# A short block packed with 128 columns, a projection moved ahead of packing, one transfer for two h0 blocks, and the last normalisation on GpSimd

## The chip, the core and the metric

The kernel runs on one core of a Trainium2 chip. The metric is the device time of that core in microseconds (us). Three runs of the kernel before the change gave 470.95, 471.35 and 472.15 us; their median is 471.35 us. A separate profiled execution took 470.71 us, of which 468.9 us lie between its first and its last instruction (its span).

## The reference, cut to what matters

Inputs: features x (5000 x 128), an adjacency matrix adj (5000 x 5000, f32, about 100 MB, zeros and ones), h0 (5000 x 128), one-hot classes y (5000 x 16), two 128 x 128 weights and two biases.

```
# layer 0
a   = adj * (y @ y.T)                     # keep edges inside a class
a   = a / max(sum(|a|, row), 1e-12)
x   = layernorm(x + 0.9 * (a @ x) + 0.1 * h0)
# layer 1
f   = tanh(adj * adj) * (adj > 0)         # a row has fewer than 350 ones: top_k keeps all
h2  = tanh(x @ W_proj + b_proj)
x   = layernorm(x + relu(f @ (h2 @ W_gcn) + b_gcn))
```

## The kernel before

The 5000 rows are 39 full blocks of 128 rows and a short one of 8 (`NB` = 40 blocks, `FULL` = 39, `LAST` = 39, `TAIL` = 8). The 5000 columns are cut in the same way. Blocks 1 to 38 come in pairs: of 256 consecutive rows, lane p holds rows 2p and 2p+1, so that block 2s+1 has the even ones and block 2s+2 the odd ones.

The adjacency is read once, in layer 0, and kept as bits. For each block of rows t, SyncE (SP) loads two halves of the row block into `a_rows` (2688 and 2312 columns, two buffers of each, L314). VectorE (DVE) casts each half to bf16 in `a_bits` (L750; one buffer of each half), ScalarE (ACT) counts its zeros (L644), and TensorE (PE) packs it: in `pack_rows` (L437) the block of 128 x 128 bits is the stationary operand and the 128 x 9 matrix `pack` moves, so that 16 rows become one 16-bit word. There are 21 such matmuls for half 0 and 19 for half 1; the last of half 1 has 8 stationary columns and not 128, since the last block of columns has 8. ACT copies the words (L661), DVE masks them with the same-class words (`same_class`, L862) and unpacks them, one bit of each byte at a time, as fp8 weights (`turned`, L839, eight instructions), and PE multiplies them by the parts of x (L487, 40 matmuls of 257 columns in two halves of 21 and 19) into `acc`.

What follows in layer 0 for a block n is: a row scale, two multiply-adds, the statistics (DVE, L880 to L908), the inverse deviation on GpSimd (POOL, `inverse_std`, L394 and L397, a power on 128 x 1), the normalisation (DVE, L851), a copy to `xs` (POOL, L410), a transpose (PE, L542), a copy of it (ACT, L695), the projection (PE, two f32 matmuls, L566), tanh (ACT, L677), and the second product (PE, L550). POOL forms 0.1 * h0 + x beforehand (`residual`, L383 and L388) from `h0_rows`, which SP loads with one transfer for each block, of 128 pieces of 512 bytes (`load_h0`, L321).

The engines run software-pipelined steps. In PE's step t (L512 to L576) the order is: first half of the product of block t-2, packing of half 0 of block t, transpose of block t-5, second product of block t-6, second half of the product of block t-2, packing of half 1 of block t, projection of block t-5. Steps 3 to 12 hold extra matmuls for the same-class words. A helper `steps` writes the first and the last steps out and runs the middle ones in a loop of two steps. SP's step t loads the rows of block t once the cast and the count of block t-2 have freed the buffer (L312, L313), and then h0 of block t-1, which waits until `residual` of block t-3 is through (L320).

Layer 1 unpacks the kept words and multiplies them by the parts of the features (L487, 40 matmuls a block), followed by the same chain to the second normalisation (`step1` of DVE, L1008 on; L851 and the store of the result at L351). Part of its first products is started early, in steps 42 to 45. At the very end each engine reads a flag (`TENSOR_LOAD`: DVE at L1358, SP at L1172) and jumps over a second, general version of the kernel that is not needed here, to the barrier at L1489.

## Time and profile before

| | value |
|---|---|
| median of three runs | 471.35 us (470.95 to 472.15) |
| profiled execution, time | 470.71 us |
| its span | 468.9 us |
| PE busy | 444.4 us, 95% of the span |
| DVE busy | 378.3 us, 81% |
| ACT busy | 266.3 us, 57% |
| POOL busy | 158.9 us, 34% |
| HBM read | 105.57 MB |
| chain that ended last | PE 88%, DVE 6%, ACT 3% |

The page cuts the span into 40 slices. The transfers run at 400 to 420 GB/s for the first 22 slices, which is layer 0, and hardly at all afterwards. So the shares of busy time over the whole span mix two stages: layer 0, to about 283 us, and layer 1, to 462 us, with a tail of 7 us. Matmuls overlap one another, so a busy PE isn't PE at its peak; how far its chain can be shortened is read from the pieces of the chain of work that ended last.

### The profile page before, as it was taken

What the parts mean: (1) busy time and instruction counts of PE and PEld (TensorE: products, weight loads), DVE (VectorE), ACT (ScalarE), POOL (GpSimd) and SP (SyncE); (2) the same over time, 40 slices, a digit from 0 to 9 for tenths busy, and PEclk for the clock granted to TensorE, in tenths of its full rate; (3) what the DMA queues carried; (4) which work ended last, traced back from release to release, by engine and by line L of the source; (5) the groups of instructions that cost most, each with busy time, mean ns of one, the idle gap of its engine ahead of it and who ended that gap; (6) DMA issues with size and microseconds to landing.
All of it is one profiled execution on the core that took longest, in us unless ns stands there. A gap on an engine that the chain in (4) does not pass through costs nothing.

```text
span 468.9 us, 15231 instructions
## 1 busy us (share of the span) xinstructions
PE 444.4 (95%) x5104; PEld 391.6 (84%) x5104; DVE 378.3 (81%) x1362; ACT 266.3 (57%) x355; POOL 158.9 (34%) x309
## 2 busy tenths in 40 slices
PE   3669999999999999999999999999999999999994
PEld 2448889899889989988998887888888888888882
DVE  5888999999999999999999956676566566566553
ACT  4998999999999999999999934900000000000000
POOL 3012543455544444555444441221221221221221
PEclk9977999999999999999999999999999999999999
DMA  8999999999999999999999100000000000000000
GB/s 266 410 413 418 416 415 408 409 396 412 420 420 419 420 421 418 421 421 419 413 418 419 32 1 1 13 12 17 17 11 17 17 11 17 17 11 16 17 17 18
DMA packets 28254, 108.50 MB, mean 231 GB/s; under 512 B 5401, under 2 KB 18226, under 8 KB 18226
## 3 DMA queue, kind: packets, MB, share of 16 engines
q1 hardware_dynamic: 28226, 108.14, 57.4%
q8 instruction: 16, 0.26, 0.2%
q14 instruction: 12, 0.10, 0.1%
HBM read 105.57 MB, written 2.56 MB: 231 GB/s over the span
## 4 chain that ended last, share of the span: by engine, by line
PE 88%; DVE 6%; ACT 3%; issue 2%; POOLq 0%; DVEq 0%; POOL 0%; ACTq 0%
PE acc L487 71%; PE words L437 9%; PE proj_acc L566 3%; PE feat_acc L550 2%; DVE a_bits L750 2%; ACT count_out L651 2%; PE xnt_acc L542 1%; DVE x_parts L779 1%; DVE g_words L300 1%; ACT count_out L720 1%; DVE turned L839 1%; ACT count_out L712 1%; PE gram_acc L469 0%; DVE y_diag L764 0%; PE words L453 0%
## 5 line engine op out<-in xcount | busy, mean ns | idle before, releaser
L487 PE MATMUL acc<-x_parts,turned 128*128 128x257 f16 (+1 forms) x1600 | 195.2, 276 | 0.7 <-DVE x_parts L779 0.7
L644 ACT ACTIVATE count_out<-a_rows,ones 128x2688 bf16<-128x2688 f32 (+1 forms) x80 | 190.0, 2375 | 0.5
L487 PEld LDWEIGHTS acc<-x_parts,turned 128*128 128x128 fp8e4 (+1 forms) x1600 | 156.9, 98 | 25.3 <-DVE x_parts L779 1.2
L487 PE MATMUL acc<-f_parts,turned 128*128 128x256 f16 (+1 forms) x1560 | 171.6, 273 | 0.8 <-DVE turned L839 0.8
L487 PEld LDWEIGHTS acc<-f_parts,turned 128*128 128x128 fp8e4 (+1 forms) x1560 | 152.0, 98 | 19.3 <-issue 1.3
L750 DVE TENSOR_SCALAR a_bits<-a_rows 128x2688 bf16<-128x2688 f32 (+1 forms) x80 | 116.6, 1458 | 2.3 <-DMA a_rows<-in_adj_dram 1.9
L394 POOL TENSOR_TENSOR var_eps<-mean_var,consts 128x1 f32<-128x1 f32 x80 | 18.5, 231 | 269.2 <-DVE mean_var L1046 139.8
L839 DVE TENSOR_SCALAR turned<-a_words 128x320 uint16 (+1 forms) x305 | 66.5, 232 | 53.2 <-PE acc L487 52.8
L397 POOL TENSOR_TENSOR rstd<-var_eps,consts 128x1 f32<-128x1 f32 x80 | 87.4, 1093 | 6.3
L839 DVE TENSOR_SCALAR turned<-same_class 128x320 uint16<-128x320 uint16 x313 | 71.7, 254 | 0.1
L437 PEld LDWEIGHTS words<-pack,a_bits 128*128 128x128 bf16 (+1 forms) x1600 | 53.8, 96 | 10.0 <-DVE a_bits L750 6.4
L437 PE MATMUL words<-pack,a_bits 128*128 128x9 bf16 (+1 forms) x1600 | 54.9, 167 | 5.2 <-DVE a_bits L750 5.2
L851 DVE TENSOR_SCALAR xn<-z,mean_var,rstd 128x128 f32<-128x128 f32 x80 | 30.4, 381 | 1.9 <-POOL rstd L397 1.0
L410 POOL COPY xs<-xn 128x128 f32 (+2 forms) x40 | 28.1, 702 | 0.4 <-DVE xn L851 0.4
L383 POOL TENSOR_TENSOR h_part<-h_rows,consts 128x128 f32<-128x128 f32 (+1 forms) x40 | 19.7, 492 | 20.4 <-DMA h_rows<-in_L_gnn_h_dram 20.2
L661 ACT ACTIVATE a_words<-words 128x360 f32 (+1 forms) x40 | 18.9, 472 | 13.3 <-PE words L437 13.2
L388 POOL TENSOR_TENSOR xh<-h_part,xs 128x128 f32<-128x128 f32 (+1 forms) x40 | 21.4, 534 | 7.4 <-POOL h_part L383 6.6
L566 PE MATMUL proj_acc<-xn_t,wp 128*128 128x128 f32 (+1 forms) x80 | 19.1, 320 | 0.2 <-issue 0.2
L1022 DVE SCALAR_TENSOR_TENSOR low_feat<-acc,consts,bg_all 128x128 f32<-128x128 f32 (+1 forms) x40 | 13.8, 344 | 4.7 <-PE acc L487 4.7
L677 ACT ACTIVATE h_t<-proj_acc,bp_col 128x128 f32<-128x128 f32 (+1 forms) x40 | 14.6, 365 | 5.2 <-PE proj_acc L566 5.2
L695 ACT ACTIVATE xn_t<-xnt_acc 128x128 f32<-128x128 f32 (+1 forms) x40 | 11.0, 275 | 10.3 <-PE xnt_acc L542 8.7
L550 PE MATMUL feat_acc<-wg,h_t 128*128 128x128 f32 (+1 forms) x80 | 15.6, 277 | 0.8 <-ACT h_t L677 0.6
(111 smaller groups left out, 287.8 us busy)
## 6 DMA issues: line engine op xcount, KB each, us to landing
a_rows<-in_adj_dram SPq DMA_DIRECT2D x39, 1344.0 KB, 8.0
a_rows<-in_adj_dram SPq DMA_DIRECT2D x39, 1156.0 KB, 8.3
h_rows<-in_L_gnn_h_dram SPq DMA_DIRECT2D x39, 64.0 KB, 5.6
out_dram<-xn SPq DMA_DIRECT2D x39, 64.0 KB, 1.5
xs<-in_x_dram SPq DMA_DIRECT2D x3, 640.0 KB, 10.3
xs<-in_x_dram SPq DMA_DIRECT2D x1, 512.0 KB, 9.0
y_nat<-in_L_gnn_y_dram SPq DMA_DIRECT2D x1, 304.0 KB, 3.6
a_rows<-in_adj_dram SPq DMA_DIRECT2D x1, 84.0 KB
```

What stands on the lines that cost most here:

```text
L383: pool.tensor_tensor(h0_part[0:m, :], h0_rows[par][0:m, :], alpha[0:m, :].to_broadcast([m, F]), ALU.mult).then_inc(s_h0part, 1)
L388: pool.tensor_tensor(xh[par][0:m, :], h0_part[0:m, :], at(xs, n, m), ALU.add)\
L397: pool.tensor_tensor(rstd[par][0:m, :], var_eps[0:m, :], neg_half[0:m, :], ALU.pow)\
L410: pool.tensor_copy(at(xs, t - 4, m), xn[par][0:m, :]).then_inc(s_kept, 1)
L437: mm = pe.matmul(words[par][0:k, b * PITCH:b * PITCH + WORDS + 1], a_bits[h][0:m, c:c + (k - 1) * d + 1:d], pack[0:m, :], start=True, stop ...
L487: mm = pe.matmul(acc[par][0:m, 0:cols], bits, parts[:, b, 0:cols], start=first and b == blocks[0], stop=last and b == blocks[-1])
L550: pe.matmul(feat_acc[0:m6, 0:F], h2_t[:, 0:m6], wg[:, :], start=True, stop=True)\
L566: pe.matmul(proj_acc[:, 0:m5], wp[:, :], xn_t[:, 0:m5], start=True, stop=True)\
L644: act.activation(count_out[0:m, 0:w], a_rows[par][h][0:m, 0:w], ACT.Relu, bias=ones[0:m, 0:1], scale=-HUGE, accum_out=col).then_inc(s_coun ...
L750: dve.tensor_scalar(a_bits[h][0:m, 0:w], a_rows[par][h][0:m, 0:w], 1.0, None, ALU.is_equal).then_inc(s_bits, 1)
L839: up = dve.tensor_scalar(turned_at(n, par)[:, :, bit * WORDS:(bit + 1) * WORDS], source, abs(shift), ONE_PAIR, op, ALU.bitwise_and)
L851: return dve.tensor_scalar(xn[par][0:m, :], z[par][0:m, :], mean_var[par][0:m, 0:1], rstd[par][0:m, :], ALU.subtract, ALU.mult)
```

## The change

Four things change.

- The last block of columns, in half 1, is packed with 128 stationary columns as the others are. The columns past the 5000th are zeros that DVE writes once into `a_bits[1]`; the memsets of the places that the short product left unwritten go, and with them a wait of PE in the setup.
- In PE's step the projection of block t-5 stands ahead of the packing of half 1 and not behind it.
- h0 of the two blocks of a pair comes with one transfer, of 128 pieces of 1 KB, into a buffer of twice the size. It is issued in even steps, and waits for `residual` of the block four before. For the buffers' names, SP and POOL run their loops four steps at a time (`steps4`).
- The last block's second normalisation is done by POOL, straight after its inverse deviation, and not by DVE.

```diff
+    def steps4(eng, step, lag, first):
+        for t in range(first):
+            step(t, t % 2, t // 2, 0, t)
+        count = (FULL - first) // 4
+        with eng.Fori(0, count) as i:
+            for c in range(first, first + 4):
+                step(i * 4 + c, c % 2, i * 2 + c // 2, i, c)
+        for t in range(first + count * 4, NB + lag):
+            step(t, t % 2, t // 2, 0, t)
...
-        h0_rows = [sb(f"h0_rows{p}", [P, F]) for p in range(2)]
+        h0_rows = [sb(f"h0_rows{p}", [P, 2, F]) for p in range(2)]
...
+            def load_h0(n, par, pair, i, c):
+                slot, _ = h0_group(i, c)
+                if not isinstance(n, int) or n >= 3:
+                    sp.wait_ge(s_xh, n - 2)
...
+                    both = h0[P:FULL * P, :].rearrange("(s p e) f -> s p (e f)", p=P, e=2)
+                    both = both[pair] if isinstance(n, int) else both[bass.ds(pair, 1), :, :].rearrange("a p c -> p (a c)")
+                    sp.dma_start(h0_rows[slot][:, :, :].rearrange("p e f -> p (e f)"), both).then_inc(s_h0[slot], 16)
...
-                if valid(t - 1) and (not isinstance(t, int) or t >= 3):
-                    load_h0(t - 1, (par + 1) % 2, pair if par == 1 else pair - 1)
-            steps(sp, step, 4)
+                if valid(t - 1) and c >= 4 and par == 0:
+                    load_h0(t - 1, 1, pair - 1, i, c - 1)
+            steps4(sp, step, 4, 5)
...
-            steps(pool, step, LAG)
+            steps4(pool, step, LAG, LAG + 2)
...
+                if isinstance(t, int) and t - 2 == LAST:
+                    m = rows_of(LAST)
+                    pool.wait_ge(s_rstd, 2 * NB)
+                    pool.wait_ge(s_out[par], (pair - 1) * 16)
+                    pool.wait_ge(s_result, LAST)
+                    pool.tensor_scalar(xn[par][0:m, :], z[par][0:m, :], mean_var[par][0:m, 0:1],
+                                       rstd[par][0:m, :], ALU.subtract, ALU.mult).then_inc(s_result, 1)
...
-                    k = rows_of(b)
                     c, d = column(b) - HALF[h].start, spacing(b)
-                    mm = pe.matmul(words[par][0:k, b * PITCH:b * PITCH + WORDS + 1],
-                                   a_bits[h][0:m, c:c + (k - 1) * d + 1:d], pack[0:m, :], start=True, stop=True)
+                    mm = pe.matmul(words[par][:, b * PITCH:b * PITCH + WORDS + 1],
+                                   a_bits[h][0:m, c:c + (P - 1) * d + 1:d], pack[0:m, :], start=True, stop=True)
...
-            pe.wait_ge(s_yp_sb, TURN + 2)
+            pe.wait_ge(s_yp_sb, TURN + 1)
...
-                if valid(t):
-                    pack_rows(t, par, rows_of(t), 1)
...
                     pe.matmul(proj_acc[:, 0:m5], wp[:, :], xn_t[:, 0:m5], start=True, stop=True)\
                         .then_inc(s_proj, 1)
+                if valid(t):
+                    pack_rows(t, par, rows_of(t), 1)
...
-            for p in range(2):
-                dve.memset(words[p][:, LAST * PITCH:NB * PITCH], 0.0)
+            dve.memset(a_bits[1][:, N - HALF[1].start:NB * P - HALF[1].start], 0.0)
...
-            dve.wait_ge(s_yp_sb, TURN + 1)
-            dve.memset(words[1][:, LAST * PITCH:NB * PITCH], 0.0).then_inc(s_yp_sb, 1)
...
-                if valid(t - 3):
+                if valid(t - 3) and not (isinstance(t, int) and t - 3 == LAST):
```

## Rows read from the trace of the kernel before

**Rows 1.** Busy time by stage; columns: stretch, length, each engine's busy us, PEclk, DMA share, GB/s

```profile
119.22:169.08 49.86, 49.86 (x671) 44.83 (x668) 49.25 (x153) 46.78 (x63) 25.05 (x41) 1.00 1.01 420
```

**Rows 2.** The chain that ended last, one step of layer 0: start us, us, what

```profile
119.05 0.53 PE words L437 x19
119.58 0.42 PE proj_acc L566 x2
120.00 2.35 PE acc L487 x21
122.34 0.51 PE words L437 x21
122.85 0.17 PE xnt_acc L542
...
123.24 2.12 PE acc L487 x19
```

**Rows 3.** DMA queue by stretch (110 to 230, 12 to 17, 300 to 400): packets, MB, share of 16 engines

```profile
q1 hardware_dynamic: 8257, 50.33, 101.4%
...
q1 hardware_dynamic: 1927, 1.93, 108.7%
...
q1 hardware_dynamic: 3168, 1.44, 4.9%
```

**Rows 4.** SP's issues in steps 22 and 38, and us to landing of their first loads

```profile
148.45 2.89 SPq L314 DMA_DIRECT2D a_rows<-in_adj_dram  x2
249.47 2.89 SPq L314 DMA_DIRECT2D a_rows<-in_adj_dram  x2
...
a_rows<-in_adj_dram SPq DMA_DIRECT2D x1, 1344.0 KB, 8.0
...
a_rows<-in_adj_dram SPq DMA_DIRECT2D x1, 1344.0 KB, 7.2
```

**Rows 5.** Timeline of DVE and PE, steps 21 to 23 and 38: start us, us, engine line

```profile
150.57 1.56 DVE L750 TENSOR_SCALAR a_bits<-a_rows 128x2688 bf16<-128x2688 f32 x1
156.57 1.55 DVE L750 TENSOR_SCALAR a_bits<-a_rows 128x2688 bf16<-128x2688 f32 x1
163.02 1.56 DVE L750 TENSOR_SCALAR a_bits<-a_rows 128x2688 bf16<-128x2688 f32 x1
257.37 1.55 DVE L750 TENSOR_SCALAR a_bits<-a_rows 128x2688 bf16<-128x2688 f32 x1
258.73 2.51 PE L487 MATMUL acc<-x_parts,turned 128*128 128x257 f16 x21
```

**Rows 6.** The chain: a projection straight behind a product, a product straight behind a packing

```profile
276.61 0.22 PE proj_acc L566 x2
...
43.56 2.45 PE acc L487 x21
```

**Rows 7.** Timeline of ACT, its copy of the transpose in the step of rows 2

```profile
123.05 0.28 ACT L695 ACTIVATE xn_t<-xnt_acc 128x128 f32<-128x128 f32 x1
```

**Rows 8.** Timeline of the tail, last work of DVE and POOL

```profile
463.43 0.17 DVE L1046 BATCH_NORM_AGGREGATE mean_var<-stats 8x2 f32<-8x6 f32 x1
463.68 0.24 POOL L394 TENSOR_TENSOR var_eps<-mean_var,consts 8x1 f32<-8x1 f32 x1 [3.59 <-DVE mean_var L1046]
464.00 0.54 POOL L397 TENSOR_TENSOR rstd<-var_eps,consts 8x1 f32<-8x1 f32 x1
464.65 0.33 DVE L851 TENSOR_SCALAR xn<-z,mean_var,rstd 8x128 f32<-8x128 f32 x1 [0.77 <-POOL rstd L397]
```

**Rows 9.** Queues at the final barrier (L1489): ns, then first and last start in us

```profile
L1489 SPq DRAIN  x1: 7/7/7, 467.6 to 467.6; - x1
L1489 DVEq DRAIN  x1: 58/58/58, 468.6 to 468.6; - x1
```

**Rows 10.** Timeline of POOL's power in steps 21 and 22

```profile
150.52 1.65 POOL L397 TENSOR_TENSOR rstd<-var_eps,consts 128x1 f32<-128x1 f32 x1
156.63 1.90 POOL L397 TENSOR_TENSOR rstd<-var_eps,consts 128x1 f32<-128x1 f32 x1
```

More of the change, by code:

```diff
@@ L108, in steps, with h0_group, h0_place @@
             step(t, t % 2, t // 2)
+    def h0_group(i, c):
+        g = (c + 1) // 2
+        return g % 2, i + g // 2
+    def h0_place(c):
+        return (c + 1) % 2 if 0 < c < LAST else 0
+    def steps4(eng, step, lag, first):
[7 more added lines that the diff above has]
+            step(t, t % 2, t // 2, 0, t)
     def valid(b):
@@ L315, in load_rows @@
                                  rows_in(adj, t, par, pair, HALF[h])).then_inc(s_rows[par][h], 16)
-            def load_h0(n, par, pair):
-                m = rows_of(n)
-                if not isinstance(n, int) or n >= 2:
-                    sp.wait_ge(s_xh, n - 1)
-                sp.dma_start(h0_rows[par][0:m, :], rows_in(h0, n, par, pair, slice(0, F))).then_inc(s_h0[par], 16)
+            def load_h0(n, par, pair, i, c):
+                slot, _ = h0_group(i, c)
+                if not isinstance(n, int) or n >= 3:
+                    sp.wait_ge(s_xh, n - 2)
+                if isinstance(n, int) and n in (0, LAST):
+                    m = rows_of(n)
+                    sp.dma_start(h0_rows[slot][0:m, 0, :], rows_in(h0, n, par, pair, slice(0, F))).then_inc(s_h0[slot], 16)
+                else:
+                    both = h0[P:FULL * P, :].rearrange("(s p e) f -> s p (e f)", p=P, e=2)
+                    both = both[pair] if isinstance(n, int) else both[bass.ds(pair, 1), :, :].rearrange("a p c -> p (a c)")
+                    sp.dma_start(h0_rows[slot][:, :, :].rearrange("p e f -> p (e f)"), both).then_inc(s_h0[slot], 16)
             sp.dma_start(pair_view(y_nat, 1, FULL), pairs_of(y, 1, FULL)).then_inc(s_in["y"], 16)
@@ L333, in _ @@
             load_rows(1, 1, 0)
-            load_h0(0, 0, 0)
-            load_h0(1, 1, 0)
+            load_h0(0, 0, 0, 0, 0)
+            load_h0(1, 1, 0, 0, 1)
             sp.dma_start(wp[:, :], w_proj).then_inc(s_in["wp"], 16)
@@ L339, in _, with step @@
             sp.dma_start(bg_row[:, :], b_gcn.rearrange("(a p) -> a p", a=1)).then_inc(s_in["bg"], 16)
-            def step(t, par, pair):
+            def step(t, par, pair, i, c):
                 if not isinstance(t, int) or t >= 2:
                     load_rows(t, par, pair)
-                if valid(t - 1) and (not isinstance(t, int) or t >= 3):
-                    load_h0(t - 1, (par + 1) % 2, pair if par == 1 else pair - 1)
-            steps(sp, step, 4)
+                if valid(t - 1) and c >= 4 and par == 0:
+                    load_h0(t - 1, 1, pair - 1, i, c - 1)
+            steps4(sp, step, 4, 5)
             def store(t, par, pair):
@@ L376, in _, with residual @@
                                base=0, pattern=[[-1, P]], channel_multiplier=1).then_inc(s_const, 1)
-            def residual(n, par, pair):
+            def residual(n, par, i, c):
                 m = rows_of(n)
-                pool.wait_ge(s_h0[par], pair * 16 + 16)
+                slot, turn = h0_group(i, c)
+                pool.wait_ge(s_h0[slot], turn * 16 + 16)
                 pool.wait_ge(s_xh, n)
-                pool.tensor_tensor(h0_part[0:m, :], h0_rows[par][0:m, :],
+                pool.tensor_tensor(h0_part[0:m, :], h0_rows[slot][0:m, h0_place(c), :],
                                    alpha[0:m, :].to_broadcast([m, F]), ALU.mult).then_inc(s_h0part, 1)
@@ L398, in inverse_std, with step @@
                     .then_inc(s_rstd, 1)
-            def step(t, par, pair):
+            def step(t, par, pair, i, c):
                 odd = (par + 1) % 2
                 if valid(t - 2):
-                    residual(t - 2, par, pair - 1)
+                    residual(t - 2, par, i, c - 2)
                 if valid(t - 3):
@@ L409, in step @@
                     pool.wait_ge(s_xn, t - 3)
+                    pool.sem_inc(s_passed, 1)
                     pool.tensor_copy(at(xs, t - 4, m), xn[par][0:m, :]).then_inc(s_kept, 1)
@@ L555, in step @@
                     products(t - 2, par, 1)
-                if valid(t):
-                    pack_rows(t, par, rows_of(t), 1)
-                if isinstance(t, int) and t == 0:
-                    for g in range(GRAMS, 2 * GRAMS):
-                        gram_words(g)
                 if valid(t - 5):
@@ L567, in step @@
                         .then_inc(s_proj, 1)
+                if valid(t):
+                    pack_rows(t, par, rows_of(t), 1)
+                if isinstance(t, int) and t == 0:
+                    for g in range(GRAMS, 2 * GRAMS):
+                        gram_words(g)
                 if isinstance(t, int) and t == NB + 2:
```

2 lines of the change are left out of this document (1 added, 1 removed).

## The prediction

> **What bounds the kernel now.** I read the busy time by stage first, then one step of the chain that ended last, then the DMA queue, and last the distance between the engines inside a step. In layer 0 everything is nearly full: PE 49.86 of 49.86 us, DVE 49.25, ACT 46.78, and the transfers at 420 GB/s with a share of 1.01 [rows 1]. The chain names PE: a step is 2.35 (21 products) + 0.51 (21 packings) + 0.17 (transpose) + 0.22 (second product) + 2.12 (19 products) + 0.53 (19 packings) + 0.42 (projection), 6.32 us with the rounding [rows 2], without a wait. But the page's "PE 95%" hides that the transfers are as full: over 120 us the queue's packets took 101.4% of 16 engines' time, 50.33 MB, 420 GB/s [rows 3]. A step loads 5000 x 128 x 4 bytes of adjacency and 65.5 KB of h0, 2.626 MB, which at 420 GB/s is 6.25 us. So PE needs 6.32 and the transfers 6.25: two bounds 0.07 us apart, and whoever speeds PE alone meets the second at once. The reader should look for that wherever one engine is named by the chain and another row of the same stage is also full.
>
> How much slack stands between the two at the end of layer 0 decides what a faster PE is worth. In step 22 the first half was issued at 148.45 and landed 8.0 later, at 156.45, and DVE's cast began at 156.57, 0.1 later [rows 4, 5]. In step 38 it was issued at 249.47 and landed 7.2 later, at 256.7; the cast began at 257.37, 0.7 later [rows 4, 5]. The transfers have gained on the engines. DVE casts a block right behind the last unpacking of the step before, and PE's next product, which needs that unpacking, began at 258.73 [rows 5], 1.36 after the cast's start; a handoff needs about 0.1, so PE stands some 1.2 us behind DVE. Those 0.7 + 1.2 = 1.9 us are all that PE can win over the landings, whatever it saves in a step.
>
> **The short block and the projection.** 21 full packings take 0.51, so 19 should take 0.46; with the short one last they take 0.53 [rows 2], and where a product follows it directly, that product's 21 take 2.45 and not 2.35 [rows 2, 6]. So the short block costs 0.07 on entering and 0.10 on leaving. The projection takes 0.42 behind the short block and 0.22 straight behind a product [rows 2, 6], where its slow f32 weight load is covered by 257 moving columns. New sequence from the end of the 19 products: 0.22 + 0.46, against 0.53 + 0.42: 0.27 us a step less. The next step's product now stands behind packings; rows show 0.10 for that behind a short one, and no row shows it behind a full one, so the bounds are 0 and 0.10 and the saving is 0.17 to 0.27. I take 0.25, since 21 full packings are followed by a transpose of 0.17 and no more. PE then needs about 6.07 a step and is no longer the bound, by either end. What the order moves: the projection waits for ACT's copy of the transpose, which in that step ends at 123.33, 2.0 before the 19 products do at 125.36 [rows 2, 7]; if that cover were gone, PE would stand on it with the packing of half 1 behind it, and DVE's next cast of that half behind the packing. The memsets and the dropped wait in the setup: 0.1 us or less, hidden by the loads that DVE waits for in steps 2 to 7; I count nothing.
>
> **h0 in pieces of 1 KB.** Between 300 and 400 us the queue carries little but 512-byte pieces: 3168 packets took 4.9% of 1600 engine-us, 78.4, or 24.7 ns on average; some are the tiny ones that announce a landing (1.44 MB are 2816 pieces of 512), so one piece costs 24.7 to 27.8. Between 12 and 17 us it carries 1 KB pieces of x: 1927 packets took 108.7% of 80, 87 us, 45.1 ns [rows 3]. Two pieces of 512 cost 49 to 56, one of 1 KB 45 to 46. I take 8 ns saved (of the bracket 3 to 11, with tiny ones priced at a third of a small piece). A pair has 128: 128 x 8 / 16 = 64 ns a pair, 19 pairs 1.2 us, bounds 0.5 and 1.6, all of it on the path because the transfers are the bound. Its wait for `residual` is one block older than now and nothing stands behind it that would be later; at 131 KB every second step it holds a row load back by 0.16 us more in one step and less in the next, inside the slack of 1.9.
> The Trainium skill (DMA: Bandwidth & Descriptors, Specifications) gives 512 bytes and more as enough for line rate, so by it the larger pieces would save nothing; the trace disagrees, with the two averages just given.
>
> **Loops of four steps.** SP and POOL leave their loops two steps earlier, at 37. SP sits waiting for ACT in each step, and a load issued 1 us late would still land behind the one in flight. I count 0, bounds 0 and +0.5.
>
> **The last normalisation.** DVE's last work is the normalisation, 464.65 to 464.98; then it reads the flag, jumps over the general version and reaches the barrier at 468.6, 3.6 later, while SP, which waits for the last store to land, is there at 467.6 [rows 8, 9]. So DVE's jump ends the kernel. Without the normalisation DVE's last work starts at 463.43 and not at 464.65; I count 1.1 of the 1.2, so that it is there at 467.5. POOL's own normalisation can start 0.08 after its power (the gap between its two operations), at 464.62; no row shows this operation on POOL. Its nearest rows are 0.24 and 0.54 [rows 8]; I take 0.45, so that it ends at 465.07 and not at 464.98, and SP arrives at 467.7. The later of 467.5 and 467.7 stands for 468.6: 0.85 less, bounds 0.5 (POOL takes 0.8) and 1.0.
>
> **The sum.** PE starts far behind and saves 0.25 for over 30 steps, 7.5 us in all; it uses 1.9 of them, and then waits for DVE, and DVE for landings. Layer 0 gains 1.9 (slack) + 1.2 (h0) + 0.25 (in step 39, where nothing is loaded any more, PE's own saving counts once again) - 0.2 (handoffs that now show) = 3.15. From step 40 on PE's chain has neither packing nor loads and moves forward as a whole, with its waits, and so does layer 1. With 0.85 for the tail: 4.0. The profiled execution took 470.71, 1.8 more than its span; it would take 466.7. It stands 0.65 under the median of the runs shown, so I forecast 471.35 - 4.0 = 467.4.
>
> **Rivals.**
> (a) *The larger pieces save nothing* (the skill's rule, or an HBM side that sets the pace): only the 1.2 goes; 468.6. For: the packets' shares overlap a little (both over 100%), so the averages aren't pure cost. Against: 385 GB/s at 1 KB is a rate (1.93 MB in 5 us), and 512 bytes in 27 ns on 16 engines is 307.
> (b) *The tail gives nothing*, because POOL's last operation is slow (over 1.3 us) or its own jump is long: 468.2. Rows for POOL speak against it.
> (c) *DVE is the next bound, and slower than today.* In step 21 the power on POOL began 0.05 before the cast and took 1.65; in step 22 it began 0.06 after the cast and took 1.90, and the step took 163.02 - 156.57 = 6.45 and not 6.00 [rows 5, 10]. If an earlier PE put DVE in the late phase in every step, layer 0 would run at 6.45 where it ran at 6.32: 0.13 x 36 = 4.7 slower, less 0.85 in the tail: 475.2. It decides from 69% of late steps ((6.32 - 6.00) / 0.45) on. Against: the two phases alternate today, mean 6.23, and a DVE that waits for a landing starts its cast later and gives the power its head start, which pushes the step back to the early phase.
> The Trainium skill (SBUF — State Buffer) says that VectorE and GpSimd share a pair of ports and that the one that starts first holds it for its whole instruction; the two rows agree, and by that rule too the order of the two starts decides.
> (d) *The transfers aren't at their limit*, PE's saving counts in full: 0.2 x 38 + 0.85 = 8.5 less, 462.9. Against: 101.4%, steady at 420 GB/s.
> That the change doesn't do what it says I leave no chance of its own: the edits are few and plain.
>
> **How the numbers follow.** Forecast as summed, 467.4: 0.58, its own range 466.3 to 468.3. (a) 0.15. (b) 0.09, (a) and (b) together 0.05, 469.4. (c) in full or in part 0.10, of which half is a mixture that ends between 469.5 and 473. (d) 0.03. Low end: the bounds 1.6 and 1.0, the saving in steps 39 and 40 counted twice: 466.0. High end: (a) and (b) together and a touch of (c): 469.9. That leaves out 0.03 + 0.03 below and about 0.10 above. 0.3% is 1.4 us, about what a measurement of this kernel can tell from no change. Faster than 469.9: 0.86; within 469.9 to 472.8: 0.08; slower: 0.06.
>
> **What would show it.** After the change: packing of half 1 in the chain at 0.46 to 0.48 and the projection at 0.22; PE with small waits for DVE's unpacking in the loop, and DVE's cast with waits for the landing, from about step 20 on; landings 6.22 apart and 420 GB/s or a little more; the first product of layer 1's full blocks some 3.2 us earlier; 1 KB pieces and 64 ns a pair fewer; DVE at the barrier near 467.5 less 3.2, SP the last one there. Wrong if the casts never wait for a landing (then DVE or PE bounds still), if POOL's power stands at 1.9 in most steps (c), if SP's issues come late at step 37, or if the tail from DVE's last statistics to the end is still 5.4 us.

## The result, and the profile after

Six runs of the changed kernel gave a median of 468.06 us (467.66 to 468.78), six of the kernel before 471.15 (470.87 to 472.15). The ratio is 0.9931, with a 95% interval of 0.9918 to 0.9944: 3.1 us less, where 4.0 were forecast. The same kernel on another chip (experiment 9) gave 467.60 beside 471.11, ratio 0.9925 (0.9913 to 0.9938), 3.5 less. The profiled execution took 467.66, 3.05 less than that of before.

The page of the changed kernel: its span, busy time by engine, and the chain that ended last.

```profile
span 465.9 us, 15131 instructions
PE 438.7 (94%) x5104; PEld 386.3 (83%) x5104; DVE 377.9 (81%) x1359; ACT 263.5 (57%) x355; POOL 161.5 (35%) x310
PE 75%; DVE 10%; ACT 5%; issue 5%; DMA 2%; POOL 2%; POOLq 0%; DVEq 0%; ACTq 0%; SPq 0%
```

The chain that was 88% PE is 75% PE, and the shares of DVE, of transfers and of "issue" have grown. Within layer 0 it still runs through PE, 99% of the stretch from 119 to 256 us, with 1.1% of "issue", so it doesn't name what PE waits for. That has to be read from distances between the engines.

Where did the 3.05 us come from? One step of layer 0, the chain that ended last, after (start us, us, what):

```profile
200.52 0.46 PE words L471 x19
200.97 0.14 issue
201.11 2.51 PE acc L521 x21
...
206.64 0.22 PE proj_acc L595 x2
206.86 0.46 PE words L471 x19
207.32 2.38 PE acc L521 x21
209.70 0.51 PE words L471 x21
210.21 0.17 PE xnt_acc L576
210.38 0.22 PE feat_acc L584 x2
210.60 2.12 PE acc L521 x19
```

The pieces of PE are as worked out: the projection 0.22 and the packing of half 1 0.46, against 0.42 and 0.53 in [rows 2]. From 206.64 on, where PE hardly waits, a step is 0.22 + 0.46 + 2.38 + 0.51 + 0.17 + 0.22 + 2.12 = 6.08 us, forecast 6.07; the product behind a full packing costs 0.03 of the bracket 0 to 0.10. The step before is longer: 0.14 of "issue", and 2.51 instead of 2.38. Two things are in this.

One is the wait for DVE's unpacked words. DVE's last unpacking ahead of the cast ends at 200.34 + 0.52 = 200.86, and the product begins at 201.11; in the next step it ends at 206.96 and the first matmul of the product starts at 207.20. The distance is 0.24 in 22 of the 24 steps from block 15 to 38, and in all 24 of experiment 9. In the kernel before it grew from 0.34 at block 15 to 1.27 at block 38, while the products started 6.31 apart in every step: PE waited for nothing and fell behind DVE. Now it starts each product as soon as DVE's words let it.

The other is PE's own. Its loop holds two steps, and behind the one at whose end it turns, the product starts later. Experiment 8 has this without the wait for the words: there the products start 6.06 and 6.30 apart by turns, 6.18 on average. So 6.08 is PE's pace in one step of two only.

DVE's last unpacking and casts of half 0 and POOL's power in the changed kernel, steps 29 to 31 (timelines, start us, us, engine line), and one stretch of 22 steps of both kernels, first after, then before (columns as in [rows 1]):

```profile
200.34 0.52 DVE L870 TENSOR_SCALAR turned<-same_class 128x320 uint16<-128x320 uint16 x3
200.87 1.56 DVE L783 TENSOR_SCALAR a_bits<-a_rows 128x2688 bf16<-128x2688 f32 x1
206.87 1.56 DVE L783 TENSOR_SCALAR a_bits<-a_rows 128x2688 bf16<-128x2688 f32 x1
213.31 1.56 DVE L783 TENSOR_SCALAR a_bits<-a_rows 128x2688 bf16<-128x2688 f32 x1
...
200.82 1.64 POOL L424 TENSOR_TENSOR rstd<-var_eps,consts 128x1 f32<-128x1 f32 x1
206.93 1.90 POOL L424 TENSOR_TENSOR rstd<-var_eps,consts 128x1 f32<-128x1 f32 x1
213.26 1.65 POOL L424 TENSOR_TENSOR rstd<-var_eps,consts 128x1 f32<-128x1 f32 x1
```

```profile
119.45:256.83 137.38, 135.86 (x1873) 121.99 (x1870) 135.72 (x420) 128.60 (x176) 68.62 (x110) 1.00 1.01 419
```

```profile
119.45:256.83 137.38, 137.38 (x1846) 123.56 (x1845) 135.51 (x414) 128.97 (x174) 67.59 (x109) 1.00 1.01 419
```

PE is busy 135.86 of 137.38 us where it was busy all the time; DVE's 135.72 are now as many. The casts are 6.00 and 6.44 apart by turns: the short step is the one in which POOL's power begins 0.05 ahead of the cast, the long one that in which it begins 0.06 behind it. What the long step loses stands in two more rows of DVE, the normalisation of the short step and that of the long one:

```profile
202.78 0.42 DVE L882 TENSOR_SCALAR xn<-z,mean_var,rstd 128x128 f32<-128x128 f32 x1
...
208.97 0.55 DVE L882 TENSOR_SCALAR xn<-z,mean_var,rstd 128x128 f32<-128x128 f32 x1
```

It begins 1.91 behind the cast's start in the short step and 2.10 in the long one, because the late power ends at 208.83, and it takes 0.13 longer beside POOL's next operations: 0.32 of the 0.44. The rest is in the unpackings right behind it.

And the first half of that step's rows has long landed. SP issued it at 198.36 and it took 7.5, so it was there at 205.9, 1.0 before the cast at 206.87:

```profile
198.36 2.77 SPq L333 DMA_DIRECT2D a_rows<-in_adj_dram  x2
...
a_rows<-in_adj_dram SPq DMA_DIRECT2D x1, 1344.0 KB, 7.5
```

The landings of the whole stretch agree. In experiment 9, the same kernel again, the rows land 6.215 apart on average from block 24 to 38, and their lead over the casts grows from 0.88 at block 18 to 1.49 at block 38. In the profile shown they land 6.20 to 6.22 apart as well, but for one pair of blocks at 6.49, and lead by 0.5 to 1.0.

So neither PE nor the transfers set the pace of the changed kernel from block 15 on. DVE does. (Before that the change gave nothing: the casts of block 16 stand at 119.22 before and 119.45 after.) The distances between the casts of half 0 say the same. They are differences of the starts in the timelines, from block 15 to block 38:

```
before  6.00 6.45 6.01 6.45 6.01 6.43 6.00 6.45 6.06 6.32 6.25 6.36 6.25 6.37 6.23 6.40 6.23 6.41 6.24 6.38 6.24 6.37 6.24
after   6.07 6.46 6.01 6.45 6.10 6.44 6.00 6.45 6.09 6.43 6.01 6.45 6.10 6.43 6.00 6.44 6.08 6.45 6.01 6.45 6.09 6.44 6.00
```

Before, the first eight distances have the pattern 6.00 and 6.45, mean 6.225; only the last fourteen have a mean of 6.306, PE's 6.32 within 0.02. So PE, slower than DVE by 0.09 a step, fell back until DVE's casts, too, had to keep to its pace, from about block 24 on. The end of the stage hung on PE all the while, since its products stood 6.31 apart without a wait from block 15 on. After, DVE's pattern goes on to the end, but at 6.245 on average (from 119.45 to 256.83, 22 steps), since every fourth distance is 0.07 to 0.10 longer than 6.00. The gain of the loop is the difference of the two paces: 6.313 (PE before) less 6.244 (DVE after), 1.5 us in 22 steps.

At step 38 the cast began at 256.83, 0.54 earlier than in [rows 5], and PE's product at 257.16, 1.57 earlier. The last block and the end of the kernel, timeline of DVE, POOL and the queues at the last barrier (L1520; for queues: ns, then first and last start):

```profile
256.83 1.55 DVE L783 TENSOR_SCALAR a_bits<-a_rows 128x2688 bf16<-128x2688 f32 x1
257.16 2.51 PE L521 MATMUL acc<-x_parts,turned 128*128 128x257 f16 x21
...
461.55 0.17 DVE L1077 BATCH_NORM_AGGREGATE mean_var<-stats 8x2 f32<-8x6 f32 x1
...
462.76 0.79 POOL L453 TENSOR_SCALAR xn<-z,mean_var,rstd 8x128 f32<-8x128 f32 x1
```

```profile
L1520 SPq DRAIN  x1: 7/7/7, 465.4 to 465.4; - x1
L1520 DVEq DRAIN  x1: 57/57/57, 465.6 to 465.6; - x1
```

The last block's last statistics began at 461.55 and not at 463.43 [rows 8], 1.88 earlier: that is the gain of all the steps. Of it 1.57 stood at step 38 already, so 0.31 came in the steps behind it. From those statistics to the end of the span it took 4.35 us and not 5.47: that is the gain of the tail, 1.12. Together 3.0, the 3.05 of the profiled executions but for their rounding.

### The profile page after: what moved, and what is told of

Read it like the earlier page. It is cut to its first block, busy times and chain, and to the rows that moved or that the text cites. A ratio compares the mean times of both kernels' runs of the same rounds, so it can differ in the third digit from the quotient of the medians.

```text
span 465.9 us, 15131 instructions
## 1 busy us (share of the span) xinstructions
PE 438.7 (94%) x5104; PEld 386.3 (83%) x5104; DVE 377.9 (81%) x1359; ACT 263.5 (57%) x355; POOL 161.5 (35%) x310
## 4 chain that ended last, share of the span: by engine, by line
PE 75%; DVE 10%; ACT 5%; issue 5%; DMA 2%; POOL 2%; POOLq 0%; DVEq 0%; ACTq 0%; SPq 0%
PE acc L521 64%; PE words L471 6%; DVE a_bits L783 3%; DMA a_rows<-in_adj_dram 2%; PE feat_acc L584 2%; PE proj_acc L595 2%; ACT count_out L685 2%; DVE turned L870 2%; PE xnt_acc L576 1%; ACT count_out L678 1%; ACT x_parts L664 1%; POOL xs L438 1%; ACT count_out L754 1%; DVE z_high L921 1%; ACT count_out L746 1%
## 5 line engine op out<-in xcount | busy, mean ns | idle before, releaser
L521 PEld LDWEIGHTS acc<-x_parts,turned 128*128 128x128 fp8e4 (+1 forms) x1600 | 154.4, 98 | 28.9 <-issue 3.8
L471 PEld LDWEIGHTS words<-pack,a_bits 128*128 128x128 bf16 (+1 forms) x1600 | 51.3, 97 | 9.7 <-DVE a_bits L783 7.8
L471 PE MATMUL words<-pack,a_bits 128*128 128x9 bf16 (+1 forms) x1600 | 51.9, 167 | 6.4 <-DVE a_bits L783 6.4
L882 DVE TENSOR_SCALAR xn<-z,mean_var,rstd 128x128 f32<-128x128 f32 x79 | 32.5, 412 | 2.6 <-POOL rstd L424 0.8
L410 POOL TENSOR_TENSOR h_part<-h_rows,consts 128x128 f32<-128x128 f32 (+1 forms) x40 | 22.2, 554 | 20.6 <-DMA h_rows<-in_L_gnn_h_dram 20.5
L438 POOL COPY xs<-xn 128x128 f32 (+2 forms) x40 | 26.1, 653 | 0.5 <-DVE xn L882 0.5
L595 PE MATMUL proj_acc<-xn_t,wp 128*128 128x128 f32 (+1 forms) x80 | 15.4, 274 | 0.2 <-issue 0.2
```

The source lines that it names most:

```text
L410: pool.tensor_tensor(h0_part[0:m, :], h0_rows[slot][0:m, h0_place(c), :], alpha[0:m, :].to_broadcast([m, F]), ALU.mult).then_inc(s_h0part, 1)
L438: pool.tensor_copy(at(xs, t - 4, m), xn[par][0:m, :]).then_inc(s_kept, 1)
L471: mm = pe.matmul(words[par][:, b * PITCH:b * PITCH + WORDS + 1], a_bits[h][0:m, c:c + (P - 1) * d + 1:d], pack[0:m, :], start=True, stop=True)
L521: mm = pe.matmul(acc[par][0:m, 0:cols], bits, parts[:, b, 0:cols], start=first and b == blocks[0], stop=last and b == blocks[-1])
L595: pe.matmul(proj_acc[:, 0:m5], wp[:, :], xn_t[:, 0:m5], start=True, stop=True)\
L882: return dve.tensor_scalar(xn[par][0:m, :], z[par][0:m, :], mean_var[par][0:m, 0:1], rstd[par][0:m, :], ALU.subtract, ALU.mult)
```

## The experiments

Ratios are to the kernel before, run beside it on the same chip, with their 95% intervals; steps are means of 22 distances between casts, from block 16 to block 38. The expectations speak of theory D (DVE is the next bound) and theory T (the transfers are).

**1. The short block alone.** The packing with 128 columns, its memset and the dropped wait:

```diff
-                mm = pe.matmul(words[par][0:k, b * PITCH:b * PITCH + WORDS + 1],
-                               a_bits[h][0:m, c:c + (k - 1) * d + 1:d], pack[0:m, :], start=True, stop=True)
+                mm = pe.matmul(words[par][:, b * PITCH:b * PITCH + WORDS + 1],
+                               a_bits[h][0:m, c:c + (P - 1) * d + 1:d], pack[0:m, :], start=True, stop=True)
```

> The kernel before with the first edit alone: the short block packed with 128 columns. Theory D (VectorE's steps alternate between 6.0 and 6.45 us, mean 6.25, and are the next bound; the landings stand 0.5 us or more ahead of the casts): PE needs about 6.16 a step, so it closes up on VectorE's unpacking; the first product of step 39 starts 0.8 to 1.6 us earlier than 265.0, and the time falls by 1.0 to 1.8 us, nearly as much as all edits of PE together. Rival T (the transfers are the next bound): the same size, but then the casts of the loop start within 0.1 us of the landing. A third reading (PE is still the bound and all it saves counts): 0.15 x 38 = 5.7 us less.

469.16 against 471.14, ratio 0.9955 (0.9941 to 0.9969), 2.0 us less. Timelines of DVE and POOL in this run:

```profile
202.16 1.56 DVE L748 TENSOR_SCALAR a_bits<-a_rows 128x2688 bf16<-128x2688 f32 x1 [0.16 <-DMA a_rows<-in_adj_dram]
208.41 1.56 DVE L748 TENSOR_SCALAR a_bits<-a_rows 128x2688 bf16<-128x2688 f32 x1 [0.17 <-DMA a_rows<-in_adj_dram]
...
208.22 1.79 POOL L397 TENSOR_TENSOR rstd<-var_eps,consts 128x1 f32<-128x1 f32 x1
```

With pieces of 512 bytes and a faster PE the casts do come to wait for the landings: 6.21 to 6.28 apart from block 19 on, most of them after a wait of 0.11 to 0.18. In a step that waits, the power starts 0.14 to 0.21 ahead of the cast and takes 1.73 to 1.80; the alternation has gone. So the landings take 6.26 a step here, and this, theory T's sign, bounds the kernel in this execution. The profile is of the longest of the six executions (470.62), in which the cast of block 15 stood 1.2 us waiting for its landing and the lead was gone early; in the others the casts may have met the landings later.

**2. The short block and the projection ahead of the packing.**

```diff
-                if valid(t):
-                    pack_rows(t, par, rows_of(t), 1)
...
                     pe.matmul(proj_acc[:, 0:m5], wp[:, :], xn_t[:, 0:m5], start=True, stop=True)\
                         .then_inc(s_proj, 1)
+                if valid(t):
+                    pack_rows(t, par, rows_of(t), 1)
```

> The kernel before with the short block at 128 columns and the projection ahead of packing. Theory D: PE's own step falls to 6.07 but VectorE holds at 6.25, so only 0.2 to 0.5 us come on top of the first edit alone, mostly in steps 39 to 41 where VectorE doesn't bound: 1.4 to 2.2 us less than before. Theory T: 1.9 us of slack used up, 2.1 to 2.5 less than before, with casts waiting for landings. If the order counts in full: 8 us less.

468.73, ratio 0.9942 (0.9928 to 0.9955), 2.4 less; steps of 6.244 on average. The two PE edits are worth 2.4, and the order adds 0.4 to the short block, less than the intervals tell apart. The distances alternate between 6.00 and 6.45 as before up to block 25; at block 26 and all even blocks behind it the cast begins 0.14 after its landing. So both theories have a part in this run: DVE's pace first, the landings' when their lead is used up.

**3. h0 alone,** the transfers of two blocks and the loops of four steps, nothing else.

```diff
...
-                if valid(t - 1) and (not isinstance(t, int) or t >= 3):
-                    load_h0(t - 1, (par + 1) % 2, pair if par == 1 else pair - 1)
-            steps(sp, step, 4)
+                if valid(t - 1) and c >= 4 and par == 0:
+                    load_h0(t - 1, 1, pair - 1, i, c - 1)
+            steps4(sp, step, 4, 5)
...
```

> The kernel before with the h0 transfers of two blocks and the loops of four steps alone. PE at 6.31 a step still bounds it. Both theories: the time stays within 0.4 us of before; the landings come earlier against the casts by up to 1.2 us at step 38 (slack of the first half about 1.5 to 1.9 and not 0.7). If the larger pieces save nothing: the slack stays at 0.7. If SP or GpSimd come late out of the longer loops: 0.5 us or more slower.

471.18 against 471.14, ratio 1.0001 (0.9991 to 1.0011). Nothing, as long as PE's chain sets the end. The lead of the landings grew to 1.05 at block 32 and not to 1.5 to 1.9, and then one late landing brought it down: at blocks 36 and 38 the casts begin 0.14 behind it.

**4. The last normalisation alone.**

```diff
-                if valid(t - 3):
+                if valid(t - 3) and not (isinstance(t, int) and t - 3 == LAST):
```

with POOL's `tensor_scalar` as in the change.

> The kernel before with GpSimd's last normalisation alone. From the last statistics of VectorE to the end 4.3 us as in the changed kernel and not 5.45: 1.1 us less in the profile, 0.8 to 1.2 in the times. If the tail's gain was luck of one execution (SP's last wait ended 1.07 us after the last piece landed before, 0.3 after): 0.3 to 0.6 us less.

470.06, ratio 0.9979 (0.9966 to 0.9991), 1.1 less. The tail of this run, timeline and queues at its barrier:

```profile
465.07 0.17 DVE L1053 BATCH_NORM_AGGREGATE mean_var<-stats 8x2 f32<-8x6 f32 x1
...
466.28 0.79 POOL L425 TENSOR_SCALAR xn<-z,mean_var,rstd 8x128 f32<-8x128 f32 x1
```

```profile
L1496 SPq DRAIN  x1: 7/7/7, 469.0 to 469.0; - x1
L1496 DVEq DRAIN  x1: 57/57/57, 469.3 to 469.3; - x1
```

From the statistics to the barrier DVE takes 4.2, against 5.2 before (463.43 to 468.6 [rows 8, 9]). POOL's normalisation takes 0.79, and DVE is still the last, 0.3 behind SP. This profile (471.36, the longest of seven) has its casts waiting for landings from block 14 to 34, 6.26 apart, although PE is as slow as before: the lead of the landings differs between executions, and with PE at 6.31 it comes back, from block 34 on.

**5 and 10. Everything but h0,** on two chips: the changed kernel with `load_h0` and the loops of two steps as before.

> The changed kernel with h0 as before (one transfer a block, pieces of 512 bytes, loops of two steps). Theory D (VectorE's alternating steps, 6.24 on average, bound the loop; the larger pieces only move the landings): within 0.4 us of the changed kernel, 3.3 to 3.6 less than before, step mean 6.24 to 6.26, casts 0.1 to 0.4 behind the landings. Theory T (the transfers bound, the larger pieces are worth 1.2): 1.2 us slower than the changed kernel.

> The changed kernel with h0 as before, once more on the same chip. VectorE's alternation at 6.24 (as in the changed kernel) and the transfers at 6.256 with small pieces are 0.01 apart, so the two times lie within 0.4 us of each other. If the first look (467.65 against 468.06) was real, the 1 KB pieces or the loops of four steps cost 0.4 us.

467.65, ratio 0.9928 (0.9915 to 0.9941), and 467.51, ratio 0.9925 (0.9913 to 0.9937). The step of experiment 5 is 6.256, with the casts of even blocks 0.14 to 0.15 behind the landings from block 18 on. The changed kernel itself did not run on that chip; on the second one it gave 467.60 (experiment 9): h0 is worth nothing here either, -0.1 us. How the two kernels of that chip come to the same time is in their distances (10 above, 9 below):

```
6.00 6.46 6.01 6.44 6.01 6.44 6.00 6.44 6.02 6.42 6.03 6.45 6.08 6.44 6.07 6.27 6.25 6.25 6.23 6.28 6.25 6.28 6.24
6.08 6.46 6.02 6.44 6.09 6.45 6.00 6.44 6.09 6.43 6.01 6.45 6.09 6.43 6.01 6.45 6.08 6.45 6.01 6.45 6.10 6.43 6.00
```

With small pieces and loops of two steps DVE goes at 6.225 until its casts have used up the landings' lead, and then at the landings' 6.26. With the large pieces, which land 6.215 apart, it never meets the landings, but every fourth step is 0.08 longer: 6.245 throughout. A step that is longer once in four shows in every kernel that has the h0 edit (3, 6 to 9, 12), and no such pattern of four in those without it (1, 2, 4, 5, 10, 11).

**9. The changed kernel again,** beside 10, 11 and 12; its numbers stand with the result. The step is 6.245 as expected, the time 0.3 under the expected span.

> The changed kernel once more, beside the three others on one chip: 467.9 to 468.3, step mean 6.24 with steps alternating between 6.44 and 6.05.

**6 and 12. The statistics moved ahead.** If DVE's collision with the power is the bound, an earlier power must help. `row_moments`, on which the power waits, goes ahead of the unpacking of two bits:

```diff
-                bits(8, 10)
                 if post:
                     row_moments(t - 3, odd, m)
-                bits(10, BITS)
+                bits(8, BITS)
```

> The changed kernel with one instruction of VectorE moved: the mean and variance ahead of the fourth unpacking pair and not behind it, so that GpSimd's power can start about 0.2 us earlier against the next cast. Theory D with the collision of power and cast as its cause: the power stands at 1.65 or less in every step, VectorE's step alternates no longer and falls to about 6.1, the transfers are the next bound at 6.22, casts start within 0.2 of the landing, and 0.7 to 1.2 us come off the changed kernel. If the alternation has another cause: the 6.44 and 6.05 stay and the time stays, or is 0.1 x 36 worse for the wait between the two instructions.

> The changed kernel with the mean and variance earlier, once more on the same chip: 0.7 to 1.1 us under the changed kernel, step mean 6.18 to 6.21, the fastest of the four.

467.21, ratio 0.9916 (0.9900 to 0.9932), and 466.20, ratio 0.9894 (0.9879 to 0.9908). On the second chip it is 1.4 under the changed kernel and 4.9 under the kernel before: the fastest version of this study. The profiled execution of run 12 took 469.61, its four others 465.98 to 466.61, so the profile shown is that of run 6; the mean steps of both agree, 6.197 and 6.202. Timelines of DVE and POOL, and the stretch of 22 steps, run 6:

```profile
200.20 1.56 DVE L783 TENSOR_SCALAR a_bits<-a_rows 128x2688 bf16<-128x2688 f32 x1
206.34 1.56 DVE L783 TENSOR_SCALAR a_bits<-a_rows 128x2688 bf16<-128x2688 f32 x1
...
200.10 1.69 POOL L424 TENSOR_TENSOR rstd<-var_eps,consts 128x1 f32<-128x1 f32 x1
206.25 1.69 POOL L424 TENSOR_TENSOR rstd<-var_eps,consts 128x1 f32<-128x1 f32 x1
```

```profile
119.70:256.04 136.34, 135.13 (x1874) 121.58 (x1871) 132.93 (x420) 128.44 (x177) 67.59 (x111) 1.00 1.01 422
```

The power now starts ahead of the cast in every step, mostly by 0.1, and then takes 1.69 (by 0.12 to 0.23 in 5 of 24 steps, and then 1.72 to 1.83); the alternation is gone and the step is 6.197, 0.048 less than in the changed kernel. It did not fall to the 6.1 expected. From block 23 on the odd blocks' casts begin 0.15 behind their landings, which come 6.21 apart, as in run 12: with DVE faster, the transfers of the large pieces are the bound. DVE's busy time fell from 135.72 to 132.93 with the same operations. Groups of DVE's instructions in the same 22 steps (busy us, mean ns, idle before), first of the changed kernel, then of run 6:

```profile
L882 DVE TENSOR_SCALAR xn<-z,mean_var,rstd 128x128 f32<-128x128 f32 x22 | 10.7, 486 | 1.2
```

```profile
L882 DVE TENSOR_SCALAR xn<-z,mean_var,rstd 128x128 f32<-128x128 f32 x22 | 9.4, 426 | 0.0
L939 DVE BATCH_NORM_AGGREGATE mean_var<-stats 128x2 f32<-128x6 f32 x22 | 4.0, 182 | 3.3 <-DVE stats L934 2.2
```

The normalisation waits 1.2 less and is 1.3 shorter in sum, and with no unpacking between them the two halves of the statistics now wait for each other, 0.15 a step, 3.3 in all (0.2 in the changed kernel). So the move isn't the best order yet; one with an unpacking between the two was not tried. The Trainium skill (SBUF — State Buffer, Who interferes with whom) says that VectorE and GpSimd share a pair of ports, and that whoever issues first holds it for its whole instruction while the other is blocked. The runs agree that the order of the two starts decides, but not on who is held: the cast keeps its 1.56 in both orders, and a power that starts up to 0.3 ahead of it doesn't finish in its 0.55, but 0.04 behind the cast's end.

**7. The changed kernel with little h0.** From the third pair on, only 8 of the 128 lanes of h0 are loaded, so that most of the transfer is gone.

```diff
+                    q = P if isinstance(n, int) and n < 5 else 8
...
+                    sp.dma_start(h0_rows[slot][0:q, :, :].rearrange("p e f -> p (e f)"), both[0:q, :])
```

> The changed kernel with 8 of the 128 lanes of h0 loaded from the third pair on (so h0 is left out of most of the result): 2.4% fewer bytes a step. Theory D: the step stays at 6.24 and the time within 0.4 us of the changed kernel, with landings drifting 1 us and more ahead of the casts. Theory T: the step falls to 6.10 to 6.15 and the time by 2 to 4 us.

467.81, ratio 0.9925 (0.9911 to 0.9940), beside 467.65 of experiment 5 on the same chip. The queue and DVE in this run (DMA queue, 110 to 230 us, as in [rows 3]; timeline):

```profile
q1 hardware_dynamic: 5647, 49.01, 100.1%
```

```profile
201.53 1.56 DVE L784 TENSOR_SCALAR a_bits<-a_rows 128x2688 bf16<-128x2688 f32 x1
207.53 1.55 DVE L784 TENSOR_SCALAR a_bits<-a_rows 128x2688 bf16<-128x2688 f32 x1
213.98 1.56 DVE L784 TENSOR_SCALAR a_bits<-a_rows 128x2688 bf16<-128x2688 f32 x1
```

Casts 6.00 and 6.45 apart, although hardly any h0 is loaded and rows land 0.7 to 1.7 ahead of them from block 20 on (at blocks 16 and 18 the casts still waited, 0.14). This run tells the two theories apart most plainly: with the transfers relieved, nothing moves, so they weren't the bound. It shows also what the queue's share is worth as a sign: it is 100.1% here, and 1.00 or 1.01 in every run, whether the casts wait for landings or not.

**8. Both,** the moved statistics and the few lanes.

> Both together: mean and variance earlier and 8 lanes of h0 (h0 left out of most of the result as well). Theory D: with VectorE's alternation and the bytes both gone the loop runs at 6.08 to 6.15 a step, PE's own 6.07 plus handoffs: 2.5 to 5 us less than the changed kernel, more than either alone. If VectorE has another floor near 6.24: no more than the fewer bytes alone give.

466.66, ratio 0.9911 (0.9896 to 0.9925), steps of 6.177: 0.9 to 1.4 less than the changed kernel's two medians where 2.5 to 5 were expected. DVE is busy for 132.56 of 135.89 us and waits 3.3 for its own statistics, so 6.177 is what it needs with the power ahead of the cast; experiment 6's 6.197 has 0.02 of landings in it. PE doesn't wait for DVE's words here, as its products begin 0.31 to 0.56 behind the last unpacking and not 0.24. The chain of this run:

```profile
205.45 0.46 PE words L472 x19
205.90 2.36 PE acc L522 x21
...
211.51 0.46 PE words L472 x19
211.96 0.10 issue
212.06 2.51 PE acc L522 x21
```

```profile
L104 PEldq COMPARE_BRANCH  x31: 76/208/243, 112.5 to 451.5; - x31
```

From 205.90 to 212.06 it is 6.16 in the chain; from first matmul to first matmul PE's steps are 6.06 and 6.30 by turns, 6.18 on average. Every second step has the "issue" and the longer product, and in the same place the branch that ends a turn of PE's loop of two steps (0.21 us from 211.49 on). In the kernel before, where the projection stood between packing and product, the products were 6.31 apart in every step. That the branch is the cause is argued from its place, not shown. So PE's own step in the new order is 6.18 and not 6.07, as near to DVE's 6.177 as can be, and this run can't tell the two apart as the bound.

**11. The moved statistics, with h0 in small pieces.**

> The changed kernel with the mean and variance earlier, but h0 as before. With VectorE's floor down at 6.18, the transfers bound at 6.255 with small pieces: casts 0.1 to 0.2 behind the landings in every step, the step mean 6.25 to 6.26, and the time that of the kernel with h0 as before without the move, within 0.3 us. So the larger pieces, worth nothing without the move, are worth 0.7 to 1.3 us with it. If they save nothing anywhere: as fast as the next one.

468.04, ratio 0.9938 (0.9926 to 0.9950). SP's issue and the landing in its step 29, then the cast of that block:

```profile
197.65 2.77 SPq L314 DMA_DIRECT2D a_rows<-in_adj_dram  x2
...
a_rows<-in_adj_dram SPq DMA_DIRECT2D x1, 1344.0 KB, 8.5
```

```profile
206.34 1.56 DVE L755 TENSOR_SCALAR a_bits<-a_rows 128x2688 bf16<-128x2688 f32 x1
```

197.65 + 8.5 is 206.15, and the cast begins 0.2 later, as in nearly every step of this run; its mean step is 6.260, as expected, and it is 0.5 slower than experiment 10, within the noise. Beside experiment 12 on the same chip the h0 edit is worth 1.8 us in the medians, more than the 0.7 to 1.3 expected, and 6.260 - 6.202 = 0.058 a step. The rows land 6.261 apart here and 6.210 apart in run 12 (blocks 24 to 38): 0.05 a step, 0.10 a pair of blocks, where 0.064 a pair was forecast. So one transfer a pair with larger pieces does save transfer time, but only a kernel whose DVE can follow gets it. Which part is the size of the pieces and which the halved number of transfers was not tried.

## Why the prediction was right, and where it was not

467.4 was forecast; 468.06 and 467.60 were measured. The sum was 4.0 against 3.05 in the profiled executions: layer 0 gave 1.3 less than forecast, the tail 0.3 more. The way the sum has layer 0 end, with PE using up its slack over the landings and all engines then waiting for transfers, is not what the changed kernel does: DVE's own pace holds it, at 6.245, and the landings run ahead. The forecast lies as near as it does in part by luck, since a bound that it left out stood close to the one that it took (6.245 and 6.22), and the tail's larger gain made up for some of the rest.

**PE's pieces: right for one step in two.** 0.25 a step; the rows give 6.32 - 6.08 = 0.24 for the step in which the loop doesn't turn. The way in which a product behind a full packing was bounded (0 to 0.10, taken near 0) gave 0.02 for a measured 0.03. Over two steps PE's own pace fell from 6.31 to 6.18 (experiment 8), 0.13 a step: "PE then needs about 6.07" was read from the pieces of one step. Nothing of the forecast hung on it, since both are less than DVE's 6.245.

**Step 39 and behind: right.** 0.25 forecast, 0.31 measured.

**The slack of 1.9: half right.** Its second part, the 1.2 us that PE stood behind DVE, was used: the product at step 38 began 1.36 behind the cast before and 0.33 after, 1.03 closer. The first part, 0.7 between landing and cast, was not; the cast kept its distance to the landing (0.72 before, 0.69 after).

**h0, 1.2: wrong as a term of this sum.** Forecast 1.2 on the path, measured 0 in two comparisons (experiment 3 against before, 9 against 10; experiment 7, with hardly any h0 at all, was no faster than 5 either), and some 1.3 to 1.8 once DVE was made faster (11 against 12). The failed step is the sentence that it all lies on the path "because the transfers are the bound". There were three bounds, not two. [Rows 1] have DVE at 49.25 of 49.86 and [rows 5] its two distances, 6.00 and 6.45; the prediction worked out their mean, 6.23, in rival (c), and the transfers' 6.25 less 0.03 a step, 6.22. It didn't put the two beside each other: 6.23 is above 6.22, so by the rows on hand DVE's own pace was at least a tie with the transfers, and no saving of the transfers could be counted whole. The 0.02 by which DVE became slower, 6.245 against 6.225, wasn't visible before. The price of the pieces itself was right: between 110 and 230 us the trace has 27 ns for a piece of 512 bytes before and 46 ns for one of 1 KB after, 8 saved for two, as taken, and the landings came 6.215 apart in experiment 9, forecast 6.22.

**The loops of four steps: mis-sized.** Counted at 0. They came with 0.07 to 0.10 us in every fourth of DVE's steps, 0.02 a step, 0.4 us in 22 steps, which takes back what the pieces give. In the longer step (from 213.31 on) POOL's addition to `xh` starts 0.18 behind the end of the multiplication ahead of it and not 0.26, and one of DVE's unpackings beside it stands at 0.52. That the two collide is argued from these spans, not shown; whether the loop or the addressing of `h0_rows` shifts POOL was not tried either. By an estimate from experiment 10 (DVE at 6.225 where it waits for nothing), and if the pattern comes from the loops, h0 in large pieces inside loops of two steps would let the changed kernel run at 6.225 instead of 6.245.

So layer 0 gave 1.88 for 3.15: 1.03 of the 1.2, 0.54 in the cast for 0.7 + 1.2 less 0.2, and 0.31 for 0.25.

**The tail: right in sign, 1.12 for 0.85, by wrong pieces.** POOL's normalisation took 0.79, not 0.45, at the far end of the bracket; SP would then have been the last, at a gain of 0.5. It wasn't, because SP reached the barrier 1.85 after the normalisation's end (463.55 to 465.4), where before it took 2.6 (464.98 to 467.6). DVE was the last in the change and in experiment 4, as late as its jump makes it. Its last work is not the statistics at 463.43, as the prediction has it, but the normalisation of block 38 right behind them, 463.54 to 463.88 before and 461.65 to 462.00 after. From there to the barrier it took 3.6 after, as the prediction has it for before, and 464.98 - 463.88 = 1.1 is the gain. Why SP's last store was through sooner stayed open.

**The rivals.** (a) is right in that the 1.2 didn't come, and wrong in its reason: the pieces do save transfer time, but DVE hides it. Its number, 468.6, is 0.5 and 1.0 from the two medians of 468.06 and 467.60, the forecast 0.7 and 0.2: the times alone don't decide between them. (b) fell, by experiment 4. (c) was right in its engine and wrong in its phase: DVE is the bound, at the alternation of 6.00 and 6.45 and not at 6.45 in every step, so the kernel became faster. (Its threshold, (6.32 - 6.00) / 0.45, is 71% and not 69%.) The two rows don't agree with the Trainium skill's rule as the prediction says: the power that started first took 1.65, not its own 0.55 (experiment 1 has that for one that starts 0.39 and more ahead). The reason given against (c), that a cast that waits for a landing pushes the power ahead, is what experiment 1 shows. (d) fell in its number; experiments 1 and 11 show the landings as a bound at 6.26 with small pieces. But the reason given against it, the share of 101.4%, doesn't carry: in experiment 7 it is 100.1% with rows landing up to 1.7 ahead.

**What would show it.** PE at 0.46 and 0.22 with small waits for the unpacking: seen. Landings 6.22 apart: seen. SP the last at the barrier, near 464.5: not seen, DVE was there last, at 465.6. The casts waiting for landings from about step 20 on: not seen in the changed kernel, only with small pieces (1, 2, 4, 5, 10, 11), with DVE made faster (6, 12) and for a few blocks in 3 and 7. The prediction had named this: "wrong if the casts never wait for a landing".

## What to carry to other kernels

When several engines and the queue are all near full, write each one's own time for a step side by side (here PE 6.31, transfers 6.25, DVE 6.23) and sum the change to the largest that is left, not to the second that comes to mind. An engine's own pace is read where it waits for nobody, as the distances of one recurring instruction over the whole stage and over whole turns of its loop, not from one step: the casts up to block 24 gave DVE's 6.225, and the pieces of one step hid the 0.24 that every second step of PE's new order has on top. Which of two engines waits for the other is read from the distance between the end of the one's work and the start of the other's: constant (0.24 here) when the second waits, growing when it falls behind. A full queue (share 1.01) says nothing of this. And an edit that relieves a resource just behind the bound is worth nothing until the bound moves, so run it again, together with the edit that moves it.

## What was not expected of the hardware

- Two starts 0.1 us apart decide an operation's length. Next to a 1.56 us cast on DVE, POOL's power on 128 x 1 took 1.64 to 1.69 when it began 0.05 to 0.10 ahead of the cast, and 1.90 when it began 0.06 behind it. What is fixed is its end: 0.04 behind the cast's end for every power that began 0.01 to 0.3 ahead of it, in all runs (even 1.92 for one that began 0.32 ahead, experiment 3), and 0.40 behind it for those that began later than the cast. With a start of 0.39 and more ahead it took 0.55 (experiment 1). Moving the statistics ahead of two bits took DVE's step from 6.245 to 6.177 where landings didn't limit it (experiment 8).
- A normalisation of 8 x 128 took 0.79 on POOL and 0.33 on DVE [rows 8].
- With the packing of half 1 last in PE's step, every second step of PE is 0.24 longer (6.06 and 6.30, experiment 8), the one at whose end its loop turns; with the f32 projection last, all are 6.31 (the kernel before). The loop's turn as the cause is argued, not shown.
- In the profile of the same loop on two chips the pattern of distances repeated to 0.02 us where DVE waits for nobody (after and experiment 9), and mean steps to 0.005 (6.197 and 6.202 in 6 and 12, where single distances differ by up to 0.1). So differences of 0.02 a step can be read from a profile, where the medians have intervals of some 0.6 us each way.
